# Summing the edge messages as three bf16 parts for all 25 buckets instead of 20

## The chip, the cores and the metric

The kernel runs on one core of a Trainium2 chip. The metric is the device time of one execution in microseconds; smaller is better. A core has a matmul engine (TensorE, PE in the profile), a vector engine (VectorE, DVE), an activation engine (ScalarE, ACT), a general engine (GpSimd, POOL) and a queue that issues the transfers (SyncE, SP). All work from on-chip memory (SBUF); matmuls write to accumulators (PSUM), which GpSimd can't read.

## The reference, cut to what matters

A graph of 3125 nodes and 103125 directed edges, sorted by destination, goes through two hyperbolic graph layers and then through a message layer. Only the last one is touched here:

```python
edge_features = jnp.concatenate([x[src], x[dst]], axis=-1)
h = jax.nn.relu(edge_features @ W1 + b1)          # one row of 128 for each edge
edge_out = h @ W2 + b2
agg = jax.ops.segment_sum(edge_out, dst, num_segments=n)
return agg / jnp.clip(counts, 1.0)[:, None]
```

The kernel uses that W1 acts on source and destination apart: with P = x W1a and Q = x W1b + b1 the message of an edge is relu(P[src] + Q[dst]), and W2 is applied after the sum over the edges of a destination.

## The kernel before, in words

The 103125 edges are worked on in 48 groups of at most 2176. Edges of a group are sorted into 25 buckets of 128 slots by their source, and all destinations of a group lie in a window of 72 nodes. Three stages follow each other: the first graph layer (which also sorts), the second graph layer, and the message layer. The change is in the third one, which starts some 690 us into the span and takes 48 steps, one for each group. `turns` writes out steps 0 and 1 and loops over pairs of the others. Buffers are held twice (index k).

A step of the third stage, engine by engine. The 25 buckets are taken in seven quads (`QUADS`: six of four buckets, 512 columns, and one of a single bucket, 128 columns).

- TensorE, `sum_step(g)`: first `spread(g + 1)`, 125 matmuls of 128 columns in bf16 (L1563 and L1565), which put P[src] + Q[dst] for each slot of the next group into PSUM, one bank for each quad. It starts once both destination one-hots of that group are made (`s_spread_set`), and quad by quad once the bank has been read. Then `sum_messages(g)`: the rows h of each bucket times a one-hot of slot against destination (72 columns), all added in one accumulator, `rs_ps`. For the first 20 buckets (`SPLIT`, quads 0 to 4) h is in three bf16 parts and takes three matmuls a bucket (L1578, 60 in all). For the last five (quads 5 and 6) h is f32 and takes two half-width f32 matmuls a bucket, recorded as four (L1583, 20 records).
- ScalarE, `relu`: for each quad relu from PSUM (L780), to bf16 as part 0 for a split quad, or to f32. After the relu of quad q comes `middle` (L773) of quad q - 1 if that one is split: a copy of the rest to bf16, part 1.
- VectorE, `add_step(g)`: `add_messages(g - 2)` (L1322) adds a finished accumulator to the result; `source_onehots(g + 1)` (L1264) compares a row of 3200 slot indices, spread over the partitions by a transfer; then `rest` (L1285) of each split quad, relu less its bf16 part, in f32, with one of the two `destination_onehots(g + 1)` (L1268) behind each of the first two; then `sum_onehots(g + 1)`: one instruction in bf16 for 20 buckets (L1275) and one in f32 for five (L1278).
- GpSimd, `low_parts`: for each split quad the rest less its middle part, to bf16, part 2 (L595). Nothing else runs there in this stage.
- SP: a transfer of the next group's source slots as soon as `source_onehots` has read the ones before, one of the destination slots after the second `destination_onehots` (it fills Cw, L457), and three small ones from the Q table.

Each engine takes its instructions in the order written. A quad thus goes relu (ACT), rest (DVE), middle (ACT), low (POOL), and then its matmuls. Ahead of the stage, P and Q are split into three bf16 parts in the same manner (L1296 to L1309), and Q is stored to a table in memory.

Of the kernel before, what the change touches and what calls it, by code (L numbers as in the profile page):

```python
# [8 lines left out]
HID = 128  # L9
# [25 lines left out]
LOOPED = NG - EARLY - 2  # L35
PRIMED = 2
QUADS = [range(b, min(b + 4, NB)) for b in range(0, NB, 4)]
SPLIT = (0, 1, 2, 3, 4)
NSPLIT = 4 * len(SPLIT)
PIECES = [slice(0, 16), slice(16, NB)]  # L40
EIGHTS = [range(b, min(b + 8, NB)) for b in range(0, NB, 8)]
OWN = 4096.0
# [18 lines left out]
def gnn_kernel(nc, x, src_t, dst_t, w_t, w0T, b0, w1T, b1, W1, eb1, W2, eb2, out):  # L61
# [5 lines left out]
    with ctx:  # L67
# [72 lines left out]
        def carve(words, dt=f32, parts=128):  # L140
# [30 lines left out]
        P3 = carve(NB * 3 * HID // 2, bf16, PN).rearrange("p (b c h) -> p b c h", c=3, h=HID)  # L171
        GP = [carve(GT * HID).rearrange("p (t h) -> p t h", h=HID) for _ in range(2)]
        early = at[0]
        Hs = [arena[:, 0:NB * HID].rearrange("p (b h) -> p b h", h=HID),
              carve(NB * HID).rearrange("p (b h) -> p b h", h=HID)]
        H0 = Hs[1][:, 0:GT, :]
# [5 lines left out]
        Os = [carve((NB - NSPLIT) * W).rearrange("p (b w) -> p b w", w=W) for _ in range(2)]  # L182
        OB = [carve(NSPLIT * HW, bf16).rearrange("p (b w) -> p b w", w=W) for _ in range(2)]
        end = at[0]
        RQ = arena[0:PN, end:end + NB * HID].rearrange("p (b h) -> p b h", h=HID)
        H3 = [carve(NSPLIT * 3 * HID // 2, bf16).rearrange("p (b c h) -> p b c h", c=3, h=HID) for _ in range(2)]
# [11 lines left out]
        RP = QF  # L198
# [69 lines left out]
        def nth(i):  # L268
# [23 lines left out]
        s_rest_set, s_mid_set, s_low_set = (counts(n) for n in ("s_rest_set", "s_mid_set", "s_low_set"))  # L292
        row_done, row_set, row_saved = (counts(n) for n in ("row_done", "row_set", "row_saved"))
        row_stored, p3_set = sem("row_stored"), sem("p3_set")

# [27 lines left out]
            for g in range(2 * TURNS, NG):  # L323
                body(g, g % 2)

        def split_slot(q):

            i = SPLIT.index(q)
            return i, slice(4 * i, 4 * i + 4)

        def from_second(g):
            return not (isinstance(g, int) and g == 0)
# [179 lines left out]
        def _(pool):  # L512
# [76 lines left out]
                pool.wait_ge(qf_stored, 16)  # L589
                any_gather(2, p_d, GP[0])  # L590

            def low(g, k, q):
                i, at_b = split_slot(q)
                pool.wait_ge(s_mid_set, nth(len(SPLIT) * g + i))
                nc.gpsimd.tensor_tensor(H3[k][:, at_b, 2, :], Hs[k][:, 4 * q:4 * q + 4, :], H3[k][:, at_b, 1, :],  # L595
                                        ALU.subtract).then_inc(s_low_set, 1)
# [11 lines left out]
        def _(sc):  # L608
# [159 lines left out]
                                     ACT.Relu).then_inc(self_set, 1)  # L768

            def middle(g, k, q):  # L770
                i, at_b = split_slot(q)
                sc.wait_ge(s_rest_set, nth(len(SPLIT) * g + i))
                nc.scalar.activation(H3[k][:, at_b, 1, :], Hs[k][:, 4 * q:4 * q + 4, :], ACT.Copy).then_inc(s_mid_set, 1)  # L773

            def relu(g, k):
                sc.wait_ge(s_sum_done, nth(g - 2))
                for q, bs in enumerate(QUADS):
# [12 lines left out]
        def _(ve):  # L790
# [480 lines left out]
            def sum_onehots(g, k):  # L1271
                ve.wait_ge(s_sum_done, nth(g - 2))
                dst = slot_dst[:, bass.ds(g, 1), :, :].rearrange("p g b d -> p (g b) d")
                pair, plain = [128, NSPLIT, HW, 2], [128, NB - NSPLIT, W]
                nc.vector.tensor_tensor(OB[k].rearrange("p b (w d) -> p b w d", d=2),  # L1275
                                        ramp1b[:, :].rearrange("p (w d) -> p w d", d=2).unsqueeze(1).broadcast_to(pair),
                                        dst[:, 0:NSPLIT, :].unsqueeze(2).broadcast_to(pair), ALU.is_equal)
                nc.vector.tensor_tensor(Os[k], ramp[:, 1:1 + W].unsqueeze(1).broadcast_to(plain),  # L1278
                                        dst[:, NSPLIT:NB, 0].unsqueeze(2).broadcast_to(plain),
                                        ALU.is_equal).then_inc(s_onehot_set, 1)  # L1280

            def rest(g, k, q):
                i, at_b = split_slot(q)
                ve.wait_ge(s_relu_set, nth(len(QUADS) * g + q))
                nc.vector.scalar_tensor_tensor(Hs[k][:, 4 * q:4 * q + 4, :], ts_ps[q], 0.0, H3[k][:, at_b, 0, :],  # L1285
                                               ALU.max, ALU.subtract).then_inc(s_rest_set, 1)

            with ve.If(fast == 1):
# [35 lines left out]
            def add_step(g, k):  # L1324
                ahead = not is_last(g)
                if from_third(g):
                    add_messages(g - 2)
                if ahead:
                    source_onehots(g + 1, 1 - k)
                for q in SPLIT:  # L1330
# [27 lines left out]
        def _(pe):  # L1358
# [190 lines left out]
            def spread(g, k):  # L1549

                pe.wait_ge(s_spread_set, nth(g))
                pe.wait_ge(qs_in[k], 24 * (g - k) + 48)
                for q, bs in enumerate(QUADS):
                    if not from_second(g):
                        pe.wait_ge(self_set, q + 1)
                    if from_second(g):
                        pe.wait_ge(s_relu_set, nth(len(QUADS) * (g - 1) + q))
                    if from_second(g) and q in SPLIT:
                        pe.wait_ge(s_rest_set, nth(len(SPLIT) * (g - 1) + SPLIT.index(q)))
                    for e, b in enumerate(bs):  # L1560
                        ps = ts_ps[q][:, e, :]
                        for part in range(3):
                            mm(ps, OTs[k][:, b, :], P3[:, b, part, :], start=(part == 0), stop=False)  # L1563
                        for a in range(2):
                            last = mm(ps, OTd[k][a][:, b, :], qs[k][:, a, :], start=False, stop=(a == 1))  # L1565
                    last.then_inc(s_t_done, 1)

            def sum_messages(g, k):
                if not (isinstance(g, int) and g == 0):
                    pe.wait_ge(rt_added, nth(g - 1))  # L1570
                pe.wait_ge(s_onehot_set, nth(g))
                for q, bs in enumerate(QUADS):
                    if q in SPLIT:
                        i, at_b = split_slot(q)
                        pe.wait_ge(s_low_set, nth(len(SPLIT) * g + i))
                        for b in range(at_b.start, at_b.stop):
                            for part in range(3):
                                mm(rs_ps, H3[k][:, b, part, :], OB[k][:, b, :], start=(b == 0 and part == 0), stop=False)  # L1578
# [57 lines left out]
```

## Time and profile before

| | before |
|---|---|
| time, median of 3 runs | 1189.39 us (1187.72 to 1190.02) |
| time of the profiled execution | 1186.87 us |
| its span | 1185.0 us |
| busy over the span | PE 1028.0, DVE 1054.7, ACT 712.7, POOL 368.7 us |
| mean granted clock of TensorE | 0.947 |

Lines of the profile give a start in us from the span's start, a duration in us, the engine, the line of the kernel, the operation and its output and inputs with their shapes, a count where several like ones stand in one line, and in brackets the idle time ahead of it with who ended it. An instruction's recorded time can begin while the one before it on the same engine still drains, so starts follow each other a little closer than durations say. POOL's spans are rougher than the others.

### The profile page before, as it was taken

The page shows a single profiled execution, that of the slowest core. Times are in us where ns is not written, and L with a number is a line of the kernel's source. Part 1 is how long each engine was busy: PE and PEld are TensorE (multiplying, and loading weights), DVE is VectorE, ACT ScalarE, POOL GpSimd, SP SyncE. Part 2 cuts the span into 40 slices and gives each one's busy share as a digit, 9 for nine tenths or more (in the row PEclk, how much of TensorE's full clock was granted, in tenths as well). Part 3 has the DMA queues.
Part 4 walks back from the last instruction along what each step waited for, and adds up shares of the span by engine and source line. Part 5 has one row for each costly group of instructions (what it writes and reads, how often), then busy time and mean ns, then how long its engine had stood idle before and what let it go on. Part 6 is the DMA issues. An engine that isn't in the chain of part 4 may idle for free.

```text
span 1185.0 us, 53692 instructions
## 1 busy us (share of the span) xinstructions
PE 1028.0 (87%) x21722; PEld 951.0 (80%) x21722; DVE 1054.7 (89%) x1448; ACT 712.7 (60%) x1933; POOL 368.7 (31%) x268
## 2 busy tenths in 40 slices
PE   3079898989898998728998599999999999999998
PEld 2058777777787877727998479999999999999997
DVE  8879999999999999785664889999999999999995
ACT  5348888888888888520002576665556555666663
POOL 7000000000000000010000037777777777777774
PEclk9569999999999999759999689999999999999999
DMA  2002323232323232579950255444544445444450
GB/s 82 0 33 100 122 95 126 95 126 95 126 95 126 95 122 99 228 284 337 411 244 18 86 172 164 162 160 152 157 156 159 158 159 161 161 161 161 161 161 29
DMA packets 44877, 169.98 MB, mean 143 GB/s; under 512 B 19440, under 2 KB 19766, under 8 KB 44827
## 3 DMA queue, kind: packets, MB, share of 16 engines
q1 hardware_dynamic: 44827, 169.28, 39.7%
q8 instruction: 36, 0.59, 0.2%
q14 instruction: 14, 0.11, 0.0%
HBM read 121.11 MB, written 48.14 MB: 143 GB/s over the span
## 4 chain that ended last, share of the span: by engine, by line
PE 51%; DVE 32%; issue 9%; DVEq 4%; ACT 2%; DMA 1%; SPq 0%; POOL 0%; ACTq 0%; POOLq 0%
PE PS L1563 17%; PE PS L1565 11%; PE PS L1578 8%; PE PS L1436 8%; DVE arena L1055 7%; DVE arena L1032 5%; DVE arena L1040 4%; DVE arena L1018 3%; PE PS L1583 3%; DVE arena L1027 2%; DVEq L361 2%; PE PS L1467 1%; DMA Cw<-slot_rows 1%; DVE arena L1047 1%; DVE aggTw L1066 1%
## 5 line engine op out<-in xcount | busy, mean ns | idle before, releaser
L595 POOL TENSOR_TENSOR arena<-arena 128x512 bf16<-128x512 f32 x240 | 342.3, 1443 | 319.6 <-ACT arena L773 319.6
L1563 PE MATMUL PS<-arena 125*128 125x128 bf16 x3600 | 344.6, 219 | 2.5 <-DVE HTw L1268 1.0
L773 ACT ACTIVATE arena<-arena 128x512 bf16<-128x512 f32 x240 | 150.8, 628 | 187.1 <-DVE arena L1285 187.1
L1563 PEld LDWEIGHTS PS<-arena 125*128 125x128 bf16 x3600 | 250.4, 97 | 9.3 <-issue 5.1
L1436 PE MATMUL PS<-arena,A 125*64 125x72 f32 x4800 | 179.3, 230 | 65.0 <-DVE aggTw L1066 38.4
L1436 PEld LDWEIGHTS PS<-arena,A 125*64 125x64 f32 x4800 | 165.4, 139 | 74.3 <-issue 49.5
L653 ACT ACTIVATE arena<-arena 128x72 bf16<-128x72 bf16 x864 | 216.9, 344 | 1.7 <-DVE arena L1040 1.7
L1285 DVE SCALAR_TENSOR_TENSOR arena<-PS,arena 128x512 f32<-128x512 f32 x240 | 159.4, 679 | 28.7 <-ACT arena L780 28.7
L780 ACT ACTIVATE arena<-PS 128x512 bf16<-128x512 f32 (+2 forms) x336 | 171.9, 547 | 0.0
L1565 PE MATMUL PS<-arena 108*128 108x128 bf16 x1200 | 167.4, 221 | 0.0
L1565 PE MATMUL PS<-arena,HTw 108*128 108x128 bf16 x1200 | 165.8, 219 | 0.0
L582 POOL MEMSET RT<- 128x3197 f32 x1 | 2.8, 2765 | 476.4 <-PE PS L1512 476.4
L1419 PE MATMUL PS<-arena 128*128 128x72 bf16 x3600 | 127.4, 199 | 0.0
L1419 PEld LDWEIGHTS PS<-arena 128*128 128x128 bf16 x3600 | 121.4, 101 | 4.9
L670 ACT ACTIVATE arena<-PS 128x504 f32<-128x504 f32 x192 | 99.7, 545 | 35.4 <-PE PS L1419 30.6
L1055 DVE TENSOR_TENSOR arena<-arena,slots 128x504 bf16<-128x504 bf16 x144 | 116.0, 855 | 0.0
L1578 PE MATMUL PS<-arena 128*128 128x72 bf16 x2880 | 101.5, 198 | 0.4 <-DVE RT L1322 0.4
L1578 PEld LDWEIGHTS PS<-arena 128*128 128x128 bf16 x2880 | 97.8, 100 | 0.6 <-DVE RT L1322 0.6
L1565 PEld LDWEIGHTS PS<-arena 108*128 108x128 bf16 x1200 | 93.1, 98 | 0.0
L1565 PEld LDWEIGHTS PS<-arena,HTw 108*128 108x128 bf16 x1200 | 92.0, 97 | 0.0
L1264 DVE TENSOR_SCALAR arena<-Bw,colp 125x3200 bf16<-125x3200 bf16 x48 | 81.3, 1693 | 8.1 <-DMA Cw<-slot_rows 7.2
L1398 PE MATMUL PS<-arena,onesb 128*128 128x416 bf16 (+15 forms) x800 | 87.3, 263 | 0.0
(195 smaller groups left out, 1388.5 us busy)
## 6 DMA issues: line engine op xcount, KB each, us to landing
adjacency<-arena SPq DMA_DIRECT2D x48, 900.0 KB, 3.6
arena<-adjacency SPq DMA_DIRECT2D x46, 900.0 KB, 8.0
Bw<-slot_rows SPq DMA_DIRECT2D x48, 800.0 KB, 4.2
Cw<-slot_rows SPq DMA_DIRECT2D x48, 700.0 KB, 4.5
arena<-q_table SPq DMA_DIRECT2D x144, 18.0 KB
q_table<-arena SPq DMA_DIRECT2D x6, 336.0 KB
slot_rows<-slot_row SPq DMA_DIRECT2D x49, 13.0 KB
x_sb<-in_x SPq DMA_DIRECT2D x1, 700.0 KB
```

The source lines that it names most:

```text
L595: nc.gpsimd.tensor_tensor(H3[k][:, at_b, 2, :], Hs[k][:, 4 * q:4 * q + 4, :], H3[k][:, at_b, 1, :], ALU.subtract).then_inc(s_low_set, 1)
L653: last = nc.scalar.activation(WD[k][:, 2, b, :], OD[:, b, :], ACT.Copy, scale=third[k][:, b:b + 1])
L670: nc.scalar.activation(AB[k][:, bs[0]:bs[-1] + 1, :], blocks_ps[c], ACT.Copy)\
L773: nc.scalar.activation(H3[k][:, at_b, 1, :], Hs[k][:, 4 * q:4 * q + 4, :], ACT.Copy).then_inc(s_mid_set, 1)
L780: nc.scalar.activation(whole, ts_ps[q], ACT.Relu).then_inc(s_relu_set, 1)
L1055: last = nc.vector.tensor_tensor(WD[k][:, c, 0:n].rearrange("p b (w d) -> p b w d", d=2), OD[:, 0:n].rearrange("p b (w d) -> p b w d", d=2 ...
L1285: nc.vector.scalar_tensor_tensor(Hs[k][:, 4 * q:4 * q + 4, :], ts_ps[q], 0.0, H3[k][:, at_b, 0, :], ALU.max, ALU.subtract).then_inc(s_rest ...
L1419: last = mm(blocks_ps[c][:, i, :], OS[k][:, b, :], WD[k][:, part, b, :], start=(part == 0), stop=(part == 2))
L1436: last = mm(sums[half, :], A[:, b, :], adjacency[0:PN, b, :], start=(b < 2), stop=(b >= NB - 2))
L1563: mm(ps, OTs[k][:, b, :], P3[:, b, part, :], start=(part == 0), stop=False)
L1565: last = mm(ps, OTd[k][a][:, b, :], qs[k][:, a, :], start=False, stop=(a == 1))
L1578: mm(rs_ps, H3[k][:, b, part, :], OB[k][:, b, :], start=(b == 0 and part == 0), stop=False)
```

## The change

`SPLIT` is gone: all seven quads are split. GpSimd makes seven low parts a group, ScalarE seven middles (the last two behind the last relu), VectorE seven rests. The f32 one-hots and f32 matmuls are gone; one bf16 instruction makes the one-hots of all 25 buckets, and TensorE does 75 matmuls a group in the sum. The buffers are laid out anew: the one-hots and one of the rests now lie where the parts of Q were, so VectorE waits for the store of Q (`q_stored`) ahead of the first `sum_onehots`. The diff, cut to what the prediction speaks of:

```diff
-SPLIT = (0, 1, 2, 3, 4)
-NSPLIT = 4 * len(SPLIT)
...
+        def quad_at(q):
+            return slice(QUADS[q][0], QUADS[q][-1] + 1)
...
             def low_parts(g, k):
                 pool.wait_ge(s_sum_done, nth(g - 2))
-                for q in SPLIT:
-                    low(g, k, q)
+                for q in range(len(QUADS)):
+                    pool.wait_ge(s_mid_set, nth(len(QUADS) * g + q))
+                    nc.gpsimd.tensor_tensor(H3[k][:, quad_at(q), 2, :], Hs[k][:, quad_at(q), :],
+                                            H3[k][:, quad_at(q), 1, :], ALU.subtract).then_inc(s_low_set, 1)
...
                     sc.wait_ge(s_t_done, nth(len(QUADS) * g + q))
-                    whole = H3[k][:, split_slot(q)[1], 0, :] if q in SPLIT else Hs[k][:, bs[0]:bs[-1] + 1, :]
-                    nc.scalar.activation(whole, ts_ps[q], ACT.Relu).then_inc(s_relu_set, 1)
-                    if q - 1 in SPLIT:
+                    nc.scalar.activation(H3[k][:, quad_at(q), 0, :], ts_ps[q], ACT.Relu).then_inc(s_relu_set, 1)
+                    if q:
                         middle(g, k, q - 1)
+                middle(g, k, len(QUADS) - 1)
...
-                pair, plain = [128, NSPLIT, HW, 2], [128, NB - NSPLIT, W]
+                pair = [128, NB, HW, 2]
                 nc.vector.tensor_tensor(OB[k].rearrange("p b (w d) -> p b w d", d=2),
                                         ramp1b[:, :].rearrange("p (w d) -> p w d", d=2).unsqueeze(1).broadcast_to(pair),
-                                        dst[:, 0:NSPLIT, :].unsqueeze(2).broadcast_to(pair), ALU.is_equal)
-                nc.vector.tensor_tensor(Os[k], ramp[:, 1:1 + W].unsqueeze(1).broadcast_to(plain),
-                                        dst[:, NSPLIT:NB, 0].unsqueeze(2).broadcast_to(plain),
-                                        ALU.is_equal).then_inc(s_onehot_set, 1)
+                                        dst.unsqueeze(2).broadcast_to(pair), ALU.is_equal).then_inc(s_onehot_set, 1)
...
             with ve.If(fast == 1):
+                ve.wait_ge(q_stored, 32 * len(QUADS))
                 sum_onehots(0, 0)
...
-                    if q in SPLIT:
-                        i, at_b = split_slot(q)
-                        pe.wait_ge(s_low_set, nth(len(SPLIT) * g + i))
...
-                    else:
-                        pe.wait_ge(s_relu_set, nth(len(QUADS) * g + q))
-                        for b in bs:
-                            for half in halves:
-                                last = mm(rs_ps[half, :], Hs[k][:, b, half], Os[k][:, b - NSPLIT, :], start=False,
-                                          stop=(b == NB - 1))
+                    pe.wait_ge(s_low_set, nth(len(QUADS) * g + q))
+                    for b in bs:
+                        for part in range(3):
+                            last = mm(rs_ps, H3[k][:, b, part, :], OB[k][:, b, :], start=(b == 0 and part == 0),
+                                      stop=(b == NB - 1 and part == 2))
```

## Rows read from the trace of the kernel before

**Rows 1.** The page's first line, and the table by stretch for 660 to 1160 us.

```profile
span 1185.0 us, 53692 instructions
...
660.00:1160.00 500.00, 491.69 (x9808) 476.02 (x9808) 462.88 (x557) 306.57 (x604) 331.37 (x232) 0.98 0.48 156
```

**Rows 2.** The timeline of DVE over one group of the third stage.

```profile
908.67 1.35 DVE L1268 TENSOR_SCALAR arena<-Cw,halfp 108x3200 bf16<-108x3200 bf16 x1
909.94 1.27 DVE L1285 SCALAR_TENSOR_TENSOR arena<-PS,arena 128x512 f32<-128x512 f32 x2
911.80 0.69 DVE L1285 SCALAR_TENSOR_TENSOR arena<-PS,arena 128x512 f32<-128x512 f32 x1 [0.58 <-ACT arena L780]
912.41 0.90 DVE L1275 TENSOR_TENSOR arena<-ramp1b,slot_dst 128x1440 bf16<-128x1440 bf16 x1
913.22 1.49 DVE L1278 TENSOR_TENSOR arena<-ramp,slot_dst 128x360 f32<-128x360 f32 x1
...
914.77 1.80 DVE L1264 TENSOR_SCALAR arena<-Bw,colp 125x3200 bf16<-125x3200 bf16 x1
916.49 0.68 DVE L1285 SCALAR_TENSOR_TENSOR arena<-PS,arena 128x512 f32<-128x512 f32 x1
...
918.65 1.34 DVE L1268 TENSOR_SCALAR HTw<-Cw,halfp 108x3200 bf16<-108x3200 bf16 x1
```

**Rows 3.** POOL's timeline there (low parts 1; 2; 2 and 3; 4).

```profile
909.49 1.55 POOL L595 TENSOR_TENSOR arena<-arena 128x512 bf16<-128x512 f32 x1 [0.32 <-ACT arena L773]
...
911.36 1.16 POOL L595 TENSOR_TENSOR arena<-arena 128x512 bf16<-128x512 f32 x1 [0.31 <-ACT arena L773]
...
911.36 2.96 POOL L595 TENSOR_TENSOR arena<-arena 128x512 bf16<-128x512 f32 x2 [0.31 <-ACT arena L773]
...
914.28 1.44 POOL L595 TENSOR_TENSOR arena<-arena 128x512 bf16<-128x512 f32 x1
```

**Rows 4.** The timeline of ACT in the same group.

```profile
912.18 0.59 ACT L780 ACTIVATE arena<-PS 128x512 f32<-128x512 f32 x1
912.66 0.63 ACT L773 ACTIVATE arena<-arena 128x512 bf16<-128x512 f32 x1
913.18 1.25 ACT L780 ACTIVATE arena<-PS 128x128 f32<-128x128 f32 x3
```

**Rows 5.** The chain that ended last, 860 to 940 us: the sum's matmuls of that group.

```profile
907.63 1.95 PE PS L1578 x60
909.58 0.78 PE PS L1583 x20
```

**Rows 6.** The timeline of DVE before GpSimd's first low part (698.20 us).

```profile
680.23 0.28 DVE L1296 TENSOR_TENSOR arena<-PS,arena 125x128 f32<-125x128 f32 x1
...
689.79 0.91 DVE L1275 TENSOR_TENSOR arena<-ramp1b,slot_dst 128x1440 bf16<-128x1440 bf16 x1 [0.54 <-DVE arena L1309]
690.61 0.52 DVE L1278 TENSOR_TENSOR arena<-ramp,slot_dst 128x360 f32<-128x360 f32 x1
695.43 1.05 DVE L1264 TENSOR_SCALAR arena<-Bw,colp 125x3200 bf16<-125x3200 bf16 x1 [4.29 <-DMA Cw<-slot_rows]
```

**Rows 7.** The timeline at the stage's end, POOL and DVE.

```profile
1166.09 5.64 POOL L595 TENSOR_TENSOR arena<-arena 128x512 bf16<-128x512 f32 x5 [0.52 <-ACT arena L773]
...
1158.51 1.35 DVE L1268 TENSOR_SCALAR HTw<-Cw,halfp 108x3200 bf16<-108x3200 bf16 x1
...
1173.54 0.23 DVE L1322 TENSOR_TENSOR RT<-RT,PS 128x72 f32 x1 [3.10 <-PE PS L1583]
```

**Rows 8.** SP's timeline: the load of Cw in that group; below, all 48 to landing.

```profile
910.29 0.33 SPq L457 DMA_DIRECT2D Cw<-slot_rows  x1
...
DMA to landing us min/median/max: 4.1/4.5/6.5
```

**Rows 9.** SP's timeline ahead of the stage, and DVE's last instruction before the one-hots.

```profile
686.95 1.40 SPq L477 DMA_DIRECT2D arena<-q_table  x3
...
688.37 0.88 DVE L1309 TENSOR_TENSOR arena<-arena 125x512 bf16<-125x512 f32 x2
```

More of the change, by code:

```diff
@@ L173, in gnn_kernel @@
         early = at[0]
+        FREE = 2 * GT * HID - 27 * HID
         Hs = [arena[:, 0:NB * HID].rearrange("p (b h) -> p b h", h=HID),
-              carve(NB * HID).rearrange("p (b h) -> p b h", h=HID)]
-        H0 = Hs[1][:, 0:GT, :]
+              arena[:, early - FREE:early - FREE + NB * HID].rearrange("p (b h) -> p b h", h=HID)]
+        H0 = carve(NB * HID).rearrange("p (b h) -> p b h", h=HID)[:, 0:GT, :]
         O0 = carve(GT * W).rearrange("p (t w) -> p t w", w=W)
@@ L181, in gnn_kernel @@
         OTs = [carve(NB * NS // 2, bf16, PN).rearrange("p (b s) -> p b s", s=NS) for _ in range(2)]
-        Os = [carve((NB - NSPLIT) * W).rearrange("p (b w) -> p b w", w=W) for _ in range(2)]
-        OB = [carve(NSPLIT * HW, bf16).rearrange("p (b w) -> p b w", w=W) for _ in range(2)]
+        OB = [arena[:, early - FREE + NB * HID + i * NB * HW:early - FREE + NB * HID + (i + 1) * NB * HW].bitcast(bf16)
+              .rearrange("p (b w) -> p b w", w=W) for i in range(2)]
         end = at[0]
-        RQ = arena[0:PN, end:end + NB * HID].rearrange("p (b h) -> p b h", h=HID)
-        H3 = [carve(NSPLIT * 3 * HID // 2, bf16).rearrange("p (b c h) -> p b c h", c=3, h=HID) for _ in range(2)]
+        RQ, RP = (arena[0:PN, end + i * NB * HID:end + (i + 1) * NB * HID].rearrange("p (b h) -> p b h", h=HID)
+                  for i in range(2))
+        H3 = [carve(NB * 3 * HID // 2, bf16).rearrange("p (b c h) -> p b c h", c=3, h=HID) for _ in range(2)]
         OT0 = [arena[0:HR, early - GT * HID * 2 + i * NB * NS // 2:early - GT * HID * 2 + (i + 1) * NB * NS // 2]
@@ L197, in gnn_kernel @@
         QF = carve(NB * HID, parts=PN).rearrange("p (b h) -> p b h", h=HID)
-        RP = QF
         G = GP[0][:, 0:GTP // 2, :].rearrange("p t (a f) -> p (t a) f", a=2)[:, 0:GT, :]
@@ L291, in gnn_kernel @@
             "s_source_set", "s_spread_set", "s_onehot_set", "s_t_done", "s_relu_set", "s_sum_done"))
-        s_rest_set, s_mid_set, s_low_set = (counts(n) for n in ("s_rest_set", "s_mid_set", "s_low_set"))
+        s_rest_set, s_mid_set, s_low_set = (counts(n) for n in (
+            "s_rest_set", "s_mid_set", "s_low_set"))
         row_done, row_set, row_saved = (counts(n) for n in ("row_done", "row_set", "row_saved"))
@@ L324, in turns @@
                 body(g, g % 2)
-        def split_slot(q):
-            i = SPLIT.index(q)
-            return i, slice(4 * i, 4 * i + 4)
+        def quad_at(q):
+            return slice(QUADS[q][0], QUADS[q][-1] + 1)
         def from_second(g):
@@ L590, in _ @@
                 any_gather(2, p_d, GP[0])
-            def low(g, k, q):
-                i, at_b = split_slot(q)
-                pool.wait_ge(s_mid_set, nth(len(SPLIT) * g + i))
-                nc.gpsimd.tensor_tensor(H3[k][:, at_b, 2, :], Hs[k][:, 4 * q:4 * q + 4, :], H3[k][:, at_b, 1, :],
-                                        ALU.subtract).then_inc(s_low_set, 1)
             def low_parts(g, k):
                 pool.wait_ge(s_sum_done, nth(g - 2))
-                for q in SPLIT:
-                    low(g, k, q)
+                for q in range(len(QUADS)):
+                    pool.wait_ge(s_mid_set, nth(len(QUADS) * g + q))
+                    nc.gpsimd.tensor_tensor(H3[k][:, quad_at(q), 2, :], Hs[k][:, quad_at(q), :],
+                                            H3[k][:, quad_at(q), 1, :], ALU.subtract).then_inc(s_low_set, 1)
             with pool.If(fast == 1):
@@ L770, in middle @@
             def middle(g, k, q):
-                i, at_b = split_slot(q)
-                sc.wait_ge(s_rest_set, nth(len(SPLIT) * g + i))
-                nc.scalar.activation(H3[k][:, at_b, 1, :], Hs[k][:, 4 * q:4 * q + 4, :], ACT.Copy).then_inc(s_mid_set, 1)
+                sc.wait_ge(s_rest_set, nth(len(QUADS) * g + q))
+                nc.scalar.activation(H3[k][:, quad_at(q), 1, :], Hs[k][:, quad_at(q), :], ACT.Copy)\
+                    .then_inc(s_mid_set, 1)
             def relu(g, k):
                 sc.wait_ge(s_sum_done, nth(g - 2))
-                for q, bs in enumerate(QUADS):
+                for q in range(len(QUADS)):
                     sc.wait_ge(s_t_done, nth(len(QUADS) * g + q))
-                    whole = H3[k][:, split_slot(q)[1], 0, :] if q in SPLIT else Hs[k][:, bs[0]:bs[-1] + 1, :]
-                    nc.scalar.activation(whole, ts_ps[q], ACT.Relu).then_inc(s_relu_set, 1)
-                    if q - 1 in SPLIT:
+                    nc.scalar.activation(H3[k][:, quad_at(q), 0, :], ts_ps[q], ACT.Relu).then_inc(s_relu_set, 1)
+                    if q:
                         middle(g, k, q - 1)
+                middle(g, k, len(QUADS) - 1)
             with sc.If(fast == 1):
@@ L1273, in sum_onehots @@
                 dst = slot_dst[:, bass.ds(g, 1), :, :].rearrange("p g b d -> p (g b) d")
-                pair, plain = [128, NSPLIT, HW, 2], [128, NB - NSPLIT, W]
+                pair = [128, NB, HW, 2]
                 nc.vector.tensor_tensor(OB[k].rearrange("p b (w d) -> p b w d", d=2),
                                         ramp1b[:, :].rearrange("p (w d) -> p w d", d=2).unsqueeze(1).broadcast_to(pair),
-                                        dst[:, 0:NSPLIT, :].unsqueeze(2).broadcast_to(pair), ALU.is_equal)
-                nc.vector.tensor_tensor(Os[k], ramp[:, 1:1 + W].unsqueeze(1).broadcast_to(plain),
-                                        dst[:, NSPLIT:NB, 0].unsqueeze(2).broadcast_to(plain),
-                                        ALU.is_equal).then_inc(s_onehot_set, 1)
+                                        dst.unsqueeze(2).broadcast_to(pair), ALU.is_equal).then_inc(s_onehot_set, 1)
             def rest(g, k, q):
-                i, at_b = split_slot(q)
                 ve.wait_ge(s_relu_set, nth(len(QUADS) * g + q))
-                nc.vector.scalar_tensor_tensor(Hs[k][:, 4 * q:4 * q + 4, :], ts_ps[q], 0.0, H3[k][:, at_b, 0, :],
+                nc.vector.scalar_tensor_tensor(Hs[k][:, quad_at(q), :], ts_ps[q], 0.0, H3[k][:, quad_at(q), 0, :],
                                                ALU.max, ALU.subtract).then_inc(s_rest_set, 1)
@@ L1329, in add_step @@
                     source_onehots(g + 1, 1 - k)
-                for q in SPLIT:
+                for q in range(len(QUADS)):
                     rest(g, k, q)
@@ L1557, in spread @@
                         pe.wait_ge(s_relu_set, nth(len(QUADS) * (g - 1) + q))
-                    if from_second(g) and q in SPLIT:
-                        pe.wait_ge(s_rest_set, nth(len(SPLIT) * (g - 1) + SPLIT.index(q)))
+                        pe.wait_ge(s_rest_set, nth(len(QUADS) * (g - 1) + q))
                     for e, b in enumerate(bs):
@@ L1572, in sum_messages @@
                 for q, bs in enumerate(QUADS):
-                    if q in SPLIT:
-                        i, at_b = split_slot(q)
-                        pe.wait_ge(s_low_set, nth(len(SPLIT) * g + i))
-                        for b in range(at_b.start, at_b.stop):
-                            for part in range(3):
-                                mm(rs_ps, H3[k][:, b, part, :], OB[k][:, b, :], start=(b == 0 and part == 0), stop=False)
-                    else:
-                        pe.wait_ge(s_relu_set, nth(len(QUADS) * g + q))
-                        for b in bs:
-                            for half in halves:
-                                last = mm(rs_ps[half, :], Hs[k][:, b, half], Os[k][:, b - NSPLIT, :], start=False,
-                                          stop=(b == NB - 1))
+                    pe.wait_ge(s_low_set, nth(len(QUADS) * g + q))
[3 more added lines that the diff above has]
+                                      stop=(b == NB - 1 and part == 2))
                 last.then_inc(s_sum_done, 1)
```

## The prediction

> **What bounds the kernel now.** I read the table by stretch first, to see which engine fills the stage that is touched: from 660 to 1160 us TensorE is busy 491.69 of 500 us at a granted clock of 0.98, VectorE 462.88, GpSimd 331.37 [rows 1]. Then the chain of work that ended last: in this stage it runs through TensorE's matmuls alone. That would say that whatever shortens TensorE shortens the kernel. The timelines of the other engines say that it isn't so simple. VectorE ends the second destination one-hots of one group at 908.67 + 1.35 = 910.02 and of the next at 918.65 + 1.34 = 919.99 [rows 2], a period of 9.97 us, and between them it is idle only 0.58 us, ahead of the rest of quad 4. TensorE ends its sum at 909.58 + 0.78 = 910.36 [rows 5], 0.34 us after the one-hots that its next spread has to wait for. The two engines turn at the same pace, and VectorE's own loop has no wait on TensorE in it. So a gain on TensorE is taken only as far as VectorE's loop gets shorter too.
>
> **What VectorE's loop is made of.** Compare its rows in the stage with the same instructions before GpSimd has work. The source one-hots take 1.80 us here and 1.05 alone; the f32 one-hots 1.49 and 0.52 [rows 2, 6]. Lay GpSimd's low parts beside them, as ends. Second destination one-hots end 910.02; low 1 ends 911.04, 1.02 later, though it is recorded from 909.49. Bf16 one-hots end 913.31; low 3 ends 914.32, 1.01 later. F32 one-hots end 914.71, 0.39 after low 3. Low 4 ends 915.72, 1.01 after them. Source one-hots end 916.57, 0.85 after low 4 [rows 2, 3]. The two engines take turns: one of these instructions of VectorE and one of GpSimd never overlap but for their start-up, and the one that asks second ends a fixed time after the first: 1.01 for a low part, 0.85 for a source or destination one-hot, 0.39 for the f32 one-hots, 0.79 for the bf16 ones (913.31 less the end of low 2, 911.36 + 1.16 = 912.52). The rests take no part in it: they keep their 0.68 with a low part beside them (911.80, inside low 2).
>
> The Trainium skill, "SBUF — State Buffer", section "Who interferes with whom", has this as a rule: VectorE and GpSimd share one pair of ports under an exclusive lock, held for a whole instruction, by VectorE in its two-port modes or with two SBUF inputs, and whoever issues first blocks the other. The trace agrees. By that rule the change is costly, since it moves work onto the shared pair; without it the change would be worth what TensorE gains, rival 1.
>
> **Part by part.** TensorE: 60 bf16 matmuls take 1.95 us, 0.0325 each; the 20 f32 records take 0.78 [rows 5]. Fifteen more bf16 ones cost 0.49, so the sum falls from 2.73 to 2.44 us, 0.29 us a group, 14 us over 48 groups if all of it is taken.
>
> ScalarE: two more middles and one f32 relu turned to bf16. It has 500 - 307 us of idle time in the stretch [rows 1], but its order matters: with a middle between them relus come 1.0 us apart (relu of quad 5 at 912.18, middle at 912.66, relu of quad 6 at 913.18 [rows 4]).
>
> VectorE: it loses the f32 one-hots and 5 buckets' worth of others join the bf16 ones; it gains a rest of 512 columns (starts 0.60 apart) and one of 128 (0.28, bound by the 128-column subtraction out of PSUM; starts 0.20 apart [rows 6]). The bf16 one-hots grow from 1440 to 1800 columns: 0.79 x 1.25 = 0.98 on the shared pair; bounds 0.79 (nothing per column) and 0.79 + 0.39 (what the f32 five cost now).
>
> GpSimd: it gains one low part of 512 columns, 1.01 on the pair and 5.64 / 5 = 1.13 from start to start [rows 7], and one of 128 columns. No row shows that one: its time on the pair lies between nothing and the full 1.01. I take 0.25, its share by columns, with 0.15 of start-up ahead (1.16 less 1.01).
>
> Demand on the shared pair, a group: before, 5 x 1.01 + 3 x 0.85 + 0.79 + 0.39 = 8.8 us of 9.97. After, 6 x 1.01 + 0.25 + 3 x 0.85 + 0.98 = 9.8. So even packed without a gap the new group can't fall much below the old 9.97.
>
> **The new group, laid out.** I keep the rows above until they change. Second destination one-hots end at 910.02. Rests 2 and 3 and middle 2 as before; lows 2, 3, 4 follow back to back, starting 911.36, 912.49 and 913.62, since low 3 no longer meets one-hots; low 4 ends at 914.78. Rest 4 at 911.80. Rest 5 can't follow at once: its relu ends at 912.18 + 0.59 = 912.77, so it runs from 912.81. Rest 6 waits for its relu (913.18 + 0.28, the 128-column cost) and runs from 913.50. The one-hots come at 913.70. Low 4 started at 913.62 and was next at the pair, so they wait for 914.78 and end 0.98 later, at 915.76. Before, they ended with no wait, and the f32 ones overlapped part of GpSimd's turn. Low 5, waiting, ends 1.01 later at 916.77. The result is added meanwhile; the source one-hots, waiting, end 0.85 later at 917.62 (before: 916.57). From there to the second destination one-hots' end it was 919.99 - 916.57 = 3.42 [rows 2]; low 6, blocked until 917.62, is done by 918.1 and ahead of the first destination one-hots' turn at about 918.3, and low 0 and low 1 fall as before. That end comes at 921.04. The period is 11.02 us, 1.05 more than 9.97.
>
> TensorE needs 9.97 - 0.29 = 9.68 and then waits 1.3 us a group for the destination one-hots. Low 6 of a group is done around 918.1, 7.7 us after the spread beside it began, while its three matmuls come 9.6 us after, so the sum doesn't wait. The slot transfer of Cw, issued 0.27 after the destination one-hots and landing 4.5 later [rows 8], comes at 914.8 and isn't needed before the source one-hots' turn at 916.8. The wait for `q_stored` is hidden: SP issues its window load, which stands behind that same wait, at 686.95, and VectorE gets there after 689.25 [rows 9]; cover lost, it would cost a microsecond or two once. Fewer columns in the first one-hots and other buffer places: nothing.
>
> The end: the old kernel begins the last group's lows at 1166.09, 6.23 after the last destination one-hots, and adds the last group at 1173.54, 1.81 after the lows' end [rows 7]. Now the first rest of that group stands behind the delayed one-hots (915.76 - 910.02 = 5.74, then the add, 0.68 of rest, 0.66 of middle), so the lows begin 7.2 after, there are 1.13 + 0.4 us more of them, and behind the last stand three matmuls, some 0.5 us, instead of 1.81: +1.0 + 1.5 - 1.3, about +1 us.
>
> **The sum.** From the first to the last destination one-hots there are 46 periods: 46 x 1.05 = 48.3, and 1 for the end: 1186.87 + 49 = 1236 us, against the profiled execution's own time; its median sister is 2.5 us (0.2%) longer, so I say 1236. That is 3.9% slower. 0.2% is about what a measurement of this kernel can tell from no change.
>
> **Rivals.**
> 1. TensorE sets the pace: the pair's turns don't cost VectorE more, each group takes 9.68 and the kernel 1186.87 - 14 = 1173 us. For it: the chain runs through TensorE alone. Against: the demand of 9.8 on the pair. It decides if new low parts slip into gaps and VectorE's loop falls under 9.7, which needs over 1.3 us of waits gone. 0.05.
> 2. The waits only move: the lost f32 one-hots pay for the rest; a period of 9.9 to 10.0, 1185 to 1190 us. For it: VectorE's own work falls, by 2.2 us of one-hots against 1.0 and 0.8. 0.05.
> 3. The one-hots reach the pair before low 4 (the margin is 0.1 us and POOL's spans are rough). They end at 913.70 + 1.09 = 914.79, low 4 at 915.80, the source one-hots at 916.65; but low 5 now stands in front of the first destination one-hots (0.3 us lost) and low 6 and low 0 in front of the second (0.4 us or more). Period about 10.8, 1186.87 + 46 x 0.8 + 1 = 1225; with fewer of these losses 10.5, 1211. 0.22.
> 4. The 128-column low part costs nearly a full one, 1.01: it ends at 918.63, holds up the destination one-hots by 0.3, period 11.3, 1250 us. 0.06.
>
> The forecast has 0.62, with a spread of 0.15 us a period, 1229 to 1243. The range takes in rival 3 and the upper ends of the costs: 1206 to 1246. Faster 0.05, same 0.05, slower 0.90.
>
> **What would show it.** One-hots of 1800 columns recorded at about 2.0 us instead of 1.1; three low parts back to back ahead of them, then one of about 2.0; source one-hots still at 1.8; destination one-hots' ends 11.0 us apart; TensorE idle over 1 us a group ahead of L1563, released by VectorE; ScalarE and the transfers never last. It would be wrong if the one-hots show 1.1 us, if the lows are far from 1.16 unblocked, or if TensorE's gaps don't appear.

## The result, and the profile after

The changed kernel takes 1233.91 us (median of 5, 1233.01 to 1238.41) against 1188.67 us of the kernel before, a ratio of 1.0387 (95% interval 1.0368 to 1.0406). Its profiled execution took 1233.01 us with a span of 1231.3 us. The forecast was 1236 us, in a range of 1206 to 1246.

The page of the changed kernel, first line and busy times, and the first of its chain:

```profile
span 1231.3 us, 53459 instructions
...
PE 1011.5 (82%) x21482; PEld 939.5 (76%) x21482; DVE 1089.7 (89%) x1496; ACT 753.2 (61%) x2029; POOL 469.8 (38%) x364
...
DVE 52%; issue 17%; PE 11%; ACT 8%; DVEq 6%; DMA 5%; SPq 1%; ACTq 0%
```

TensorE is 16.5 us less busy than before, as its lighter sum promises, and the kernel is 46 us longer. The shares above are of the whole span. From 800 to 1120 us the chain was TensorE's matmuls for 99.8% before and holds none of them now: it runs through VectorE, with ScalarE's middles and relus (L767 9.3%, L774 4.0%) and a transfer of Cw in some groups (10.1%) in it. GpSimd doesn't stand in it, since the chain follows semaphores, and a turn between two engines isn't one. A group of the third stage on VectorE (start, duration, engine, line, operation; the one-hots of the sum are L1270 here, the source one-hots L1259, the destination ones L1263, the rests L1276):

```profile
939.64 1.35 DVE L1263 TENSOR_SCALAR HTw<-Cw,halfp 108x3200 bf16<-108x3200 bf16 x1
940.90 1.27 DVE L1276 SCALAR_TENSOR_TENSOR arena<-PS,arena 128x512 f32<-128x512 f32 x2
942.76 0.69 DVE L1276 SCALAR_TENSOR_TENSOR arena<-PS,arena 128x512 f32<-128x512 f32 x1 [0.58 <-ACT arena L774]
943.77 0.98 DVE L1276 SCALAR_TENSOR_TENSOR arena<-PS,arena 128x512 f32<-128x512 f32 x2 [0.31 <-ACT arena L774]
944.66 2.01 DVE L1270 TENSOR_TENSOR arena<-ramp1b,slot_dst 128x1800 bf16<-128x1800 bf16 x1
946.59 0.21 DVE L1313 TENSOR_TENSOR RT<-RT,PS 128x72 f32 x1
946.73 1.81 DVE L1259 TENSOR_SCALAR arena<-Bw,colp 125x3200 bf16<-125x3200 bf16 x1
...
950.62 1.34 DVE L1263 TENSOR_SCALAR arena<-Cw,halfp 108x3200 bf16<-108x3200 bf16 x1
```

Its second destination one-hots end at 940.99 and 951.96, 10.97 us apart (before 9.97, rows 2). Over 28 periods between 800 and 1120 us the mean is 10.99, against 9.99 in the kernel before.

GpSimd in the same group (low parts 2 to 4 in one line, then low 5, then low 6):

```profile
942.32 3.39 POOL L595 TENSOR_TENSOR arena<-arena 128x512 bf16<-128x512 f32 x3 [0.32 <-ACT arena L767]
...
945.67 2.01 POOL L595 TENSOR_TENSOR arena<-arena 128x512 bf16<-128x512 f32 x1
...
947.65 1.18 POOL L595 TENSOR_TENSOR arena<-arena 128x128 bf16<-128x128 f32 x1
```

The same one-hots ahead of the stage, with nothing beside them:

```profile
688.84 1.09 DVE L1270 TENSOR_TENSOR arena<-ramp1b,slot_dst 128x1800 bf16<-128x1800 bf16 x1 [0.61 <-DVE arena L1300]
```

Read the ends. Low 4 ends at 945.71. The one-hots, begun at 944.66, end at 946.67, 0.96 after it. Low 5 ends at 947.68, 1.01 after them. The source one-hots end at 948.54, 0.86 after low 5. Low 6 ends at 948.83, 0.29 after those. The first three of these handovers lie in VectorE's loop (low 6 doesn't hold it up), where rows 2 and 3 had the f32 one-hots, low 4 and the source one-hots. They account for the longer group. The low part that they start behind ends 4.72 us after the second destination one-hots (low 4, at 945.71) instead of 4.30 (low 3, at 914.32), and the three take 0.96 + 1.01 + 0.86 = 2.83 instead of 0.39 + 1.01 + 0.85 = 2.25: 0.42 + 0.58 = 1.00 us. From the source one-hots' end to the next second destination one-hots' end it is 3.42 in both kernels.

What TensorE shows is the wait at the start of each spread, and the waits of the stage from 720 to 1190 us say how much there is (in total, times, longest):

```profile
941.36 0.33 PE L1554 MATMUL PS<-arena 125*128 125x128 bf16 x3 [1.34 <-DVE HTw L1263]
```

```profile
PE PS L1554 <- DVE HTw L1263: 29.8, 22, 1.7
PE PS L1554 <- DVE arena L1263: 27.1, 21, 1.3
```

43 waits of 1.3 us for the destination one-hots: the gain of 14 us on TensorE's side is there, and spent waiting.

The whole difference adds up. The first of the second destination one-hots end at 699.29 instead of 700.21 (-0.9), the last at 1204.65 instead of 1159.86, so the 46 periods between are 505.4 instead of 459.7 us (+45.7), and from there to the last group's addition it is 15.1 instead of 13.7 (+1.5): 46.3, the difference of the spans.

### The profile page after: what moved, and what is told of

Read it like the earlier page. It is cut to its first block, busy times and chain, and to the rows that moved or that the text cites. A ratio compares the mean times of both kernels' runs of the same rounds, so it can differ in the third digit from the quotient of the medians.

```text
span 1231.3 us, 53459 instructions
## 1 busy us (share of the span) xinstructions
PE 1011.5 (82%) x21482; PEld 939.5 (76%) x21482; DVE 1089.7 (89%) x1496; ACT 753.2 (61%) x2029; POOL 469.8 (38%) x364
## 4 chain that ended last, share of the span: by engine, by line
DVE 52%; issue 17%; PE 11%; ACT 8%; DVEq 6%; DMA 5%; SPq 1%; ACTq 0%
PE PS L1428 8%; DVE arena L1259 7%; DVE arena L1050 6%; DVE arena L1276 6%; DVE arena L1027 5%; DVE HTw L1263 5%; DVE arena L1263 4%; DMA Cw<-slot_rows 4%; ACT arena L767 4%; DVE arena L1035 4%; DVEq L360 3%; DVE arena L1013 3%; DVE arena L1022 2%; ACT arena L774 2%; PE PS L1459 1%
## 5 line engine op out<-in xcount | busy, mean ns | idle before, releaser
L595 POOL TENSOR_TENSOR arena<-arena 128x512 bf16<-128x512 f32 (+1 forms) x336 | 442.8, 1342 | 266.5 <-ACT arena L767 266.4
L767 ACT ACTIVATE arena<-arena 128x512 bf16<-128x512 f32 (+1 forms) x336 | 190.5, 580 | 194.0 <-DVE arena L1276 190.5
L1276 DVE SCALAR_TENSOR_TENSOR arena<-PS,arena 128x512 f32<-128x512 f32 (+1 forms) x336 | 206.2, 626 | 43.7 <-ACT arena L774 43.7
L774 ACT ACTIVATE arena<-PS 128x512 bf16<-128x512 f32 (+1 forms) x336 | 176.2, 539 | 0.0
L1567 PE MATMUL PS<-arena 128*128 128x72 bf16 x3600 | 124.9, 198 | 2.7 <-DVE RT L1313 2.7
L1411 PE MATMUL PS<-arena 128*128 128x72 bf16 x3600 | 126.9, 199 | 0.0
L1411 PEld LDWEIGHTS PS<-arena 128*128 128x128 bf16 x3600 | 120.9, 101 | 4.9
L1567 PEld LDWEIGHTS PS<-arena 128*128 128x128 bf16 x3600 | 121.2, 100 | 2.8 <-DVE RT L1313 2.8
L1270 DVE TENSOR_TENSOR arena<-ramp1b,slot_dst 128x1800 bf16<-128x1800 bf16 x48 | 95.6, 1992 | 0.6 <-DVE arena L1300 0.6
L1259 DVE TENSOR_SCALAR arena<-Bw,colp 125x3200 bf16<-125x3200 bf16 x48 | 85.2, 1775 | 6.2 <-DMA Cw<-slot_rows 6.2
```

The source lines that it names most:

```text
L595: nc.gpsimd.tensor_tensor(H3[k][:, quad_at(q), 2, :], Hs[k][:, quad_at(q), :], H3[k][:, quad_at(q), 1, :], ALU.subtract).then_inc(s_low_se ...
L767: nc.scalar.activation(H3[k][:, quad_at(q), 1, :], Hs[k][:, quad_at(q), :], ACT.Copy)\
L774: nc.scalar.activation(H3[k][:, quad_at(q), 0, :], ts_ps[q], ACT.Relu).then_inc(s_relu_set, 1)
L1259: nc.vector.tensor_scalar(OTs[k].rearrange("p b s -> p (b s)"), src_bc[0:PN, :], colp[0:PN, :], None, ALU.is_equal).then_inc(s_source_set, 1)
L1276: nc.vector.scalar_tensor_tensor(Hs[k][:, quad_at(q), :], ts_ps[q], 0.0, H3[k][:, quad_at(q), 0, :], ALU.max, ALU.subtract).then_inc(s_res ...
L1411: last = mm(blocks_ps[c][:, i, :], OS[k][:, b, :], WD[k][:, part, b, :], start=(part == 0), stop=(part == 2))
```

## The experiments

All eight start from the changed kernel. Their ratios are to the kernel before, run beside them.

| kernel | what differs from the changed kernel | us | ratio (95%) | period, us |
|---|---|---|---|---|
| before | | 1188.7 | 1 | 9.99 |
| changed | | 1233.9 | 1.0387 (1.0368 to 1.0406) | 10.99 |
| sum_short | 34 matmuls a group fewer | 1234.8 | 1.0400 (1.0381 to 1.0418) | 10.98 |
| low_tiny | low parts of 2 columns | 1170.1 | 0.9855 (0.9825 to 0.9884) | 9.64 |
| low_write | low parts replaced by a subtraction of 2 columns a bucket and a fill | 1236.7 | 1.0423 (1.0395 to 1.0451) | 11.04 |
| low_five | no low 5 and 6, so 5 matmuls a group fewer | 1198.9 | 1.0092 (1.0072 to 1.0111) | 10.22 |
| dest_late | order of VectorE | 1198.5 | 1.0093 (1.0062 to 1.0124) | 10.20 |
| order_only | another order of VectorE | 1197.1 | 1.0072 (1.0047 to 1.0098) | 10.20 |
| low2_only | low 2 on VectorE | 1252.4 | 1.0545 (1.0522 to 1.0567) | 11.32 |
| mix2 | both of the last two | 1170.8 | 0.9866 (0.9839 to 0.9893) | 9.64 |

The period is the mean distance between source one-hots from 800 to 1120 us. In the expectations, "the theory" is that VectorE and GpSimd take turns at a shared pair of ports and that the queue at it, in the order in which they come, sets the period.

**Is TensorE out of it?** (sum_short)

```diff
+                    parts = 3 if q < 2 else 1
                     for b in bs:
-                        for part in range(3):
+                        for part in range(parts):
```

> The changed kernel with 41 instead of 75 matmuls in the sum: the middle and low parts of quads 2 to 6 are made but left out of the sum. Theory: TensorE waits over 1 us a group for VectorE's destination one-hots, so 34 x 0.0325 = 1.1 us less work a group changes nothing but the very end: 1232 to 1234 us. Rival D (TensorE still sets the pace in the changed kernel, as its chain did before): 1234 - 46 x 1.1 = 1183 us.

It took 1234.8 us, the changed kernel's time within a microsecond, with TensorE busy 356.07 of the 430 us from 700 to 1130. Its granted clock there was 0.94 of the full 2.4 GHz in the mean (1.00 in the changed kernel from 700 to 1190), and not even that shows in the time. Rival D falls.

**Is it VectorE's and ScalarE's longer queues?** (low_tiny)

```diff
-                    nc.gpsimd.tensor_tensor(H3[k][:, quad_at(q), 2, :], Hs[k][:, quad_at(q), :],
-                                            H3[k][:, quad_at(q), 1, :], ALU.subtract).then_inc(s_low_set, 1)
+                    nc.gpsimd.tensor_tensor(H3[k][:, quad_at(q), 2, 0:2], Hs[k][:, quad_at(q), 0:2],
+                                            H3[k][:, quad_at(q), 1, 0:2], ALU.subtract).then_inc(s_low_set, 1)
...
-                            last = mm(rs_ps, H3[k][:, b, part, :], OB[k][:, b, :], ...
+                            last = mm(rs_ps, H3[k][:, b, min(part, 1), :], OB[k][:, b, :], ...
```

> GpSimd's low parts keep their number and place but cover 2 of 128 columns of each bucket; the third matmul of each bucket takes the middle part again, so the count of matmuls is unchanged and the low parts are left out of the result. Theory (VectorE and GpSimd take turns): with hardly anything to wait for, VectorE's loop falls to about 9.0 us and TensorE's 9.68 sets the pace: 1234 - 46 x (10.98 - 9.68) = 1174 us; the one-hots of 1800 columns record about 1.1 us instead of 2.0, the source one-hots about 1.05 instead of 1.8. Rival A (the longer queues of VectorE and ScalarE themselves, seven rests and seven middles, are the cost): period still about 11, 1230 us or more. Rival B (GpSimd is simply too busy, with no turns): also about 1174, so this run doesn't part B from the theory; low_write does.

1170.1 us: VectorE and ScalarE have all their new instructions and the kernel is 64 us shorter than the changed one. Rival A falls. VectorE in low_tiny, where each one-hot takes what it takes alone and VectorE waits for TensorE instead:

```profile
943.50 1.10 DVE L1270 TENSOR_TENSOR arena<-ramp1b,slot_dst 128x1800 bf16<-128x1800 bf16 x1 [0.63 <-PE PS L1567]
...
945.15 1.05 DVE L1259 TENSOR_SCALAR arena<-Bw,colp 125x3200 bf16<-125x3200 bf16 x1
```

Its chain is TensorE's alone, at a mean period of 9.64. So this is also what the change's other half is worth once nothing of it is lost to waiting: 16 us against the kernel before, 0.35 us a group where I had 0.29 (why is said below, under the term that was off).

**GpSimd busy, or GpSimd reading?** (low_write)

```diff
-                    nc.gpsimd.tensor_tensor(H3[k][:, quad_at(q), 2, :], Hs[k][:, quad_at(q), :],
-                                            H3[k][:, quad_at(q), 1, :], ALU.subtract).then_inc(s_low_set, 1)
+                    pool.wait_ge(s_low_set, nth(len(QUADS) * g + q - 1))
+                    nc.gpsimd.tensor_tensor(H3[k][:, quad_at(q), 2, 0:2], Hs[k][:, quad_at(q), 0:2],
+                                            H3[k][:, quad_at(q), 1, 0:2], ALU.subtract)
+                    nc.gpsimd.memset(dstT[:, 0:150 if q == 6 else 580].bitcast(bf16), 0.0).then_inc(s_low_set, 1)
```

> GpSimd keeps about its time for each low part, but spends it on a fill that writes elsewhere and reads nothing (with a 2-column subtraction ahead of it); the third matmul takes the middle part again, so the low parts are left out of the result. Rival B (GpSimd too busy): still about 11.0 us a group, 1230 us. Theory: the two kinds of VectorE instruction part. By the Trainium skill, page SBUF - State Buffer, section Who interferes with whom, an instruction with two SBUF inputs meets only a GpSimd instruction that reads, one in a two-port mode meets any. If turns are taken for the read side alone in the sum's one-hots, they record about 1.1 us and the source and destination one-hots still up to 1.8: a period of about 10.2, 1234 - 0.8 x 46 = 1197 us. If a writing GpSimd instruction holds them all, all is as in the changed kernel, 1230; if it holds none, 1174.

The rows part the two kinds of instruction as expected; the time didn't follow. VectorE and GpSimd in low_write:

```profile
945.11 1.08 DVE L1272 TENSOR_TENSOR arena<-ramp1b,slot_dst 128x1800 bf16<-128x1800 bf16 x1
...
946.25 1.85 DVE L1261 TENSOR_SCALAR arena<-Bw,colp 125x3200 bf16<-125x3200 bf16 x1
...
948.62 1.39 DVE L1265 TENSOR_SCALAR arena<-Cw,halfp 108x3200 bf16<-108x3200 bf16 x1
...
950.52 1.95 DVE L1265 TENSOR_SCALAR arena<-Cw,halfp 108x3200 bf16<-108x3200 bf16 x1
```

```profile
944.26 1.07 POOL L598 MEMSET dstT<- 128x1160 bf16 x1
945.48 0.78 POOL L596 TENSOR_TENSOR arena<-arena 128x8 bf16<-128x8 f32 x1
946.20 1.06 POOL L598 MEMSET dstT<- 128x1160 bf16 x1
```

The sum's one-hots (two inputs from SBUF) run their 1.08 us from 945.11 to 946.19 beside a fill that lasts to 945.33, and keep only the reading 8-column subtraction behind it waiting, until 946.26. The source and destination one-hots wait for fills as they do for low parts: 1.85 from 946.25, ending 0.84 after the fill that ends at 947.26. So a writing GpSimd instruction doesn't stop the first kind and does stop the second, as the Trainium skill, "SBUF — State Buffer", section "Who interferes with whom", has it. The 0.93 us saved there came back at the destination one-hots, which take 1.39 and 1.95 here and 1.04 and 1.34 in the changed kernel, 0.96 more: the stand-in, with its subtraction and its own wait, leaves GpSimd hardly ever idle (387.97 of 430 us busy from 700 to 1130), so the fills reach into their place. The run settles which instructions meet; that its time is near the changed kernel's is read here as a coincidence of those two halves and not as a sign for rival B, which low_five answers.

**What the two new low parts do** (low_five)

```diff
-                for q in range(len(QUADS)):
+                for q in range(5):
                     pool.wait_ge(s_mid_set, nth(len(QUADS) * g + q))
```

> The changed kernel without the low parts of quads 5 and 6 (left out of the result; those buckets are summed in two parts). GpSimd has its old five low parts, VectorE and ScalarE their new seven rests and middles. Theory: the one-hots of the sum still stand behind low 4 (about 2.0 us recorded), but nothing is queued behind them on GpSimd, so the source one-hots take 1.05 instead of 1.8: the period falls by about 0.75 to 10.2, 1200 us. Rival A (VectorE's and ScalarE's own queues): no change, 1234. Rival B (GpSimd's amount of work alone): the old 9.97 or TensorE's pace, 1187 or less.

1198.9 us at a period of 10.22. The one-hots and the source one-hots in low_five:

```profile
947.85 2.01 DVE L1270 TENSOR_TENSOR arena<-ramp1b,slot_dst 128x1800 bf16<-128x1800 bf16 x1
...
949.93 1.04 DVE L1259 TENSOR_SCALAR arena<-Bw,colp 125x3200 bf16<-125x3200 bf16 x1
```

The wait behind low 4 is still whole (2.01), the one behind low 5 is gone (1.04 instead of 1.81). GpSimd has its old five parts and is idle for 4.0 us a group (3.40 of it in one gap), and still the kernel is 0.9% slower than before: rival B, GpSimd's amount of work alone, falls. The five matmuls that are missing don't matter: TensorE waits 28.9 us for the destination one-hots in 40 groups. Of the 45 us, about 35 hang on the two added low parts through that one wait. The other 10 us fit a loss ahead of them, which no run takes by itself: with rests 5 and 6 in front and 0.31 us of waiting for a relu, the sum's one-hots begin 3.67 us after the second destination one-hots' end instead of 2.39, and so stand behind low 4, where before they had slipped in without a wait (0.90, rows 2).

**The same work in another order** (dest_late and order_only)

```diff
-                    if ahead and q < 2:
-                        last = destination_onehots(1 - k, q)
-                    if ahead and q == 1:
-                        last.then_inc(s_spread_set, 1)
+                    if ahead and q == 0:
+                        destination_onehots(1 - k, 0)
+                    if ahead and q == 2:
+                        destination_onehots(1 - k, 1).then_inc(s_spread_set, 1)
```

> The same instructions as the changed kernel in another order on VectorE: the second destination one-hots stand behind the third rest instead of the second. Theory: what costs is who stands behind whom at the shared pair. Laid out by the same turns, the period falls from 10.98 to about 10.2, near the 9.8 us of work at the pair with start-ups: 1234 - 46 x 0.77 = 1199 us, still slower than before. Rival A (amount of work on VectorE and ScalarE): no change, 1234. Rival C (the later one-hots hold TensorE up): slower than 1234.

> The order of VectorE's instructions of mix2, with all seven low parts on GpSimd, nothing left out. Theory: order alone gives what the shared pair lets through, about 10.2 us a group as in dest_late, 1199 us: slower than before, since the pair is full. If mix2's 1171 came from the order alone, this gives about 1171 too.

1198.5 and 1197.1 us. The diff above is dest_late's. In order_only VectorE goes rest 0, rest 1, source one-hots, rest 2, destination one-hots, rest 3, destination one-hots, rests 4 to 6, one-hots of the sum.

In dest_late one instruction, moved behind one more rest, gives back 35 us, with all work the same. There the sum's one-hots wait half as long, and GpSimd's records, the waits for its turn among them, leave no gap in the 15 us shown, nor, in either order, in the 320 us from 800 to 1120. That is what a full pair looks like:

```profile
949.94 1.53 DVE L1270 TENSOR_TENSOR arena<-ramp1b,slot_dst 128x1800 bf16<-128x1800 bf16 x1
```

```profile
939.18 15.17 POOL L595 TENSOR_TENSOR arena<-arena 128x512 bf16<-128x512 f32 x10
```

The two orders differ and end at the same period, 10.20. That fits a floor, the 9.8 us of work at the pair and the start-ups between; that no order could do better was worked out, not tried.

**Less work at the pair, in either order** (low2_only and mix2)

```diff
+            def low_here(g, k):
+                ve.wait_ge(s_mid_set, nth(len(QUADS) * g + 2))
+                nc.vector.tensor_tensor(H3[k][:, quad_at(2), 2, :], Hs[k][:, quad_at(2), :],
+                                        H3[k][:, quad_at(2), 1, :], ALU.subtract).then_inc(s_low_here, 1)
...
-                for q in range(len(QUADS)):
+                for q in [q for q in range(len(QUADS)) if q != 2]:
                     pool.wait_ge(s_mid_set, nth(len(QUADS) * g + q))
```

> The changed kernel's order on VectorE, with the low part of quad 2 made by VectorE behind rest 4 instead of by GpSimd, nothing left out. Theory: less work at the pair doesn't help in the wrong order. Laid out by turns: the moved low part stands behind GpSimd's low 3, and the rests and one-hots behind it shift later, into lows 4 and 5; the period is about 11.3, 1234 + 46 x 0.35 = 1250 us. If only the amount of work at the pair counts (9.3 us instead of 9.8), it is faster than 1234 by 20 or more.

> All 25 buckets in three bf16 parts, but the low part of quad 2 is made by VectorE (0.6 us at the pair instead of 1.01, and none on GpSimd), and VectorE's order is rest 0, rest 1, source one-hots, rest 2, destination one-hots, rest 3, destination one-hots, rest 4, low part of quad 2, rest 5, rest 6, one-hots of the sum. Theory: work at the pair falls to 9.3 us and each of VectorE's one-hots meets GpSimd after a rest; the period is 9.6 to 9.8, TensorE's 9.68 sets the pace: 1234 - 46 x 1.3 = 1174 to 1180 us, faster than the kernel before. Rival A (amount of work on VectorE): VectorE has 0.6 us more, so 1234 or more.

low2_only takes 1252.4 us, 18.5 more than the changed kernel, though it asks some 0.5 us less of the pair. The moved low part comes just after GpSimd's next one has begun, and a subtraction that takes VectorE 0.68 us with the pair free (125x512, L1300, ahead of the stage) takes 1.66 (low2_only, VectorE, then GpSimd; low parts 3 and 4 are one line):

```profile
940.73 1.66 DVE L1317 TENSOR_TENSOR arena<-arena 128x512 bf16<-128x512 f32 x1
```

```profile
940.69 2.72 POOL L595 TENSOR_TENSOR arena<-arena 128x512 bf16<-128x512 f32 x2 [1.33 <-ACT arena L767]
```

The two starts lie 0.04 us apart, and VectorE, the later one, waits a whole turn; what it would be the other way round wasn't tried. With the order of order_only, which alone gives 1197, the same move gives 1170.8 us: 63 us less than the changed kernel and 1.3% less than the kernel before. Neither half does it. In mix2 the source one-hots come when the pair is free and the sum's one-hots wait 0.16 instead of 0.92:

```profile
943.83 1.04 DVE L1317 TENSOR_TENSOR arena<-arena 128x512 bf16<-128x512 f32 x1
...
945.59 1.25 DVE L1270 TENSOR_TENSOR arena<-ramp1b,slot_dst 128x1800 bf16<-128x1800 bf16 x1
...
948.11 1.03 DVE L1259 TENSOR_SCALAR arena<-Bw,colp 125x3200 bf16<-125x3200 bf16 x1
```

At 9.64 us a group it is as fast as low_tiny, where hardly a turn is left to wait for. TensorE is busy 426.24 of the 430 us from 700 to 1130, and VectorE 428.13. It leaves nothing out and is the kernel to keep.

## Why the prediction was right

**What bounds the kernel before.** That TensorE's chain hid a loop of VectorE of the same length was the step that mattered. low_tiny shows the one side of it (with the waits gone, TensorE's 16 us are taken), the changed kernel the other. The trace of before says more than the prediction read from it: the loops weren't two that happened to be equal. Over 42 groups the first matmul of a spread starts 0.32 to 0.44 us after the second destination one-hots end; in the changed kernel, where TensorE plainly waits for them, it is 0.34 to 0.43, and in mix2, where it is seldom held up by them, 0.35 to 1.24. So VectorE set the pace already, with TensorE's wait too short to show in its chain.

**The turns.** The fixed times after the other engine's end were read from one group (rows 2 and 3). After: 0.96 for one-hots of 1800 columns (0.98 forecast, within 0.79 to 1.18), 1.01 for a low part (1.01), 0.86 for the source one-hots (0.85), 0.29 for the 128-column low part (0.25). Rival 4, which wanted 1.01 for that one, is out, and so is rival 3: low 4 got its turn first in every group from 720 to 1150 us, where the sum's one-hots take 2.01 or 2.02 us each. The forecast was partly lucky there: as laid out low 4 was ahead by 0.08 us, POOL's spans are rough, and nothing read before the run could settle who came first. Rivals 1 and 2, with periods of 9.68 and of 9.9 to 10.0, fall with the 10.99.

**The laid-out group.** 11.02 us against 10.97 in the group shown and 10.99 in the mean. The mean before is 9.99, not the 9.97 of the one group I took, so the difference was 0.99 and not 1.05: that is the largest error, 48.3 us forecast where 45.7 were measured. The end cost 1.5 instead of 1. The start of the stage came 0.9 us earlier than before, which I hadn't forecast; its cause is open.

**Engines costed at nothing.** ScalarE's order delayed rests 5 and 6 as laid out (0.31 idle ahead of them, by L774). But the sign that ScalarE is never last didn't hold: lows 2 to 4 run back to back from 942.32 because middle 2 (L767, 941.61 to 942.24) ends only then, so that middle lies in the loop, as it did in the layout, and the chain has 13.3% of ScalarE from 800 to 1120 us. TensorE waits 1.3 us a group, as forecast. No engine waits for the transfer of Cw in the changed kernel from 720 to 1190 us: the chain passes over it at 941.14, but 4.46 us later it has landed, at 945.60, 1.07 before the sum's one-hots end. In dest_late, where the second destination one-hots and so the transfer come later, it ends 35 waits of the source one-hots from 720 to 1130 us, 11.6 us in all; behind them these still take 1.16 to 1.62 us instead of 1.04, so GpSimd's turn ends later yet. The wait for `q_stored` cost nothing: SP's window load, behind the same wait, is issued at 685.99 and the first one-hots start at 688.84, 0.61 us after the last split, where it was 0.54.

**The term that was off.** With the waits gone a group is 0.35 us shorter than before (low_tiny and mix2 9.64 against 9.99), not 0.29. The sum by itself was forecast well: from the start of its first matmul to that of its last it takes 2.40 instead of 2.66 us, 0.26 less. The other 0.09 fit the short wait on VectorE that TensorE had before. It made no difference to the forecast, since nothing of it is taken.

## What to carry to other kernels

When two engines have the same period, the chain shows one of them, and here it wasn't the one that set the pace; lay out the other's loop before spending anything there. If two engines share a resource in turns, add up what a period asks of it, then write down who comes when: a start 0.04 us after the other engine's cost a whole turn in low2_only, and one instruction moved past a neighbour was worth 35 us here with all work unchanged. An instruction that runs longer in a stage than by itself is the row to look for.

## What the runs showed of the hardware

That low_write would part the two kinds of VectorE instruction was expected from the section of the Trainium skill cited there; the numbers are this case's. Beside a GpSimd fill of 1160 columns that only writes, a comparison with both inputs in SBUF takes 1.08 us, as alone (1.09), and one with a single input over 3200 bf16 columns takes up to 1.95 instead of 1.04.

Two things weren't expected. GpSimd needs 1.01 us at the pair for a subtraction of 128 x 512 elements where VectorE does one of 125 x 512 in 0.68 in all, so handing it to GpSimd can hold VectorE up for longer than doing it would take. And the turns are so regular that a layout by hand from one group gave the period of three further kernels within 0.1 us (low_five 10.2 and 10.22, dest_late 10.2 and 10.20, low2_only 11.3 and 11.32, the forecast first). order_only has 10.20 too, but its forecast of 10.2 leaned on dest_late; in low_tiny (9.68 and 9.64) and mix2 (9.6 to 9.8 and 9.64) the forecast was TensorE's pace. The miss is low_write, 10.2 and 11.04, whose stand-in changed when GpSimd comes.
